# Another order of the setup work of a cross-attention and FFN kernel: first q product between the halves of the DCA keys, head products ahead of the DCA scales, output bias and DCA values further back

## What is computed

```python
def _ln(t, w, b):
    m = jnp.mean(t, axis=-1, keepdims=True)
    v = jnp.var(t, axis=-1, keepdims=True)
    return (t - m) * jax.lax.rsqrt(v + 1e-6) * w + b

# y = ctx_1024; the last 16 of its 128 tokens are the "DCA" tokens
kv_dca = (y_dca @ Wkv_dca + bkv_dca).reshape(b, 16, 2, H, HD)
k_dca, v_dca = _ln(kv_dca[:, :, 0], kn_dca_w, kn_dca_b), kv_dca[:, :, 1]
q = _ln((x @ Wq + bq).reshape(b, s1, H, HD), qn_w, qn_b)      # x: layernorm of the input
kv = concatenate([y_main @ Wk + bk, y_main @ Wv + bv]).reshape(b, s2, H, 2 * HD)
k, v = _ln(kv[..., :HD], kn_w, kn_b), kv[..., HD:]
ctx = softmax(q k^T * HD**-0.5) v  +  softmax(q k_dca^T * HD**-0.5) v_dca
x = x_in + ctx @ Wo + bo
# FFN: activations, kernel (per column) and bias fake-quantised to 8 bits
y = relu(xq @ kq + bq);  out = x + fake_quant(y)              # xq: layernorm(x), quantised per row
```

## Time and profile before

| | us |
|---|---|
| median of 3 runs | 368.0 (364.89 to 369.49) |
| the profiled execution | 367.36 |
| its span on the core | 365.6 |
| PE busy | 320.0 (88%) |
| VectorE (DVE) busy | 314.6 (86%) |
| ScalarE (ACT) busy | 222.5 (61%) |
| GpSimd (POOL) busy | 173.3 (47%) |
| mean granted TensorE clock | 0.966 |

### The profile page before, as it was taken

One profiled execution on the slowest core, in us unless ns is written; L12 is line 12 of the kernel. 1 busy time (PEld: TensorE's weight loads), 2 busy tenths in 40 slices (PEclk: granted clock), 3 DMA queues, 4 the chain that ended last, 5 costly groups with the idle time before them and its releaser, 6 DMA issues.

```text
span 365.6 us, 7583 instructions
## 1 busy us (share of the span) xinstructions
PE 320.0 (88%) x2338; PEld 258.6 (71%) x2353; DVE 314.6 (86%) x804; ACT 222.5 (61%) x444; POOL 173.3 (47%) x261
## 2 busy tenths in 40 slices
PE   1499889799999999999999999999999999797732
PEld 0345557688878888888888888888888888595620
DVE  2987999899989999999999989999989898946664
ACT  3357986466666767676667666767676756542401
POOL 5301512337373838373738382828282827251620
PEclk9999999899999999999999999999999999959985
DMA  7870368526171919182919091919291809070002
GB/s 267 254 281 1 70 138 146 120 58 136 31 162 43 180 42 178 43 168 55 179 40 182 27 195 33 186 35 155 68 185 35 151 16 163 25 122 2 29 0 86
DMA packets 36451, 39.14 MB, mean 107 GB/s; under 512 B 8760, under 2 KB 27452, under 8 KB 36412
## 3 DMA queue, kind: packets, MB, share of 16 engines
q1 hardware_dynamic: 36044, 38.40, 48.9%
q10 hardware_dynamic: 368, 0.27, 0.3%
HBM read 17.15 MB, written 4.72 MB: 60 GB/s over the span
## 4 chain that ended last, share of the span: by engine, by line
PE 49%; DMA 10%; SPq 8%; issue 6%; ACT 3%; DVE 3%; POOL 0%; ACTq 0%; DVEq 0%
PE bank L1328 24%; DMA q_stack<-q_lo 10%; SPq L376 8%; PE bank L1445 7%; PE bank L1414 4%; PE bank L1601 4%; PE bank L1611 2%; PE bank L1425 2%; PE bank L1426 2%; PE bank L1468 2%; PE bank L1498 2%; ACT k_hi L611 1%; PE bank L1460 1%; DVE finals L1050 1%; PE bank L1503 1%
## 5 line engine op out<-in xcount | busy, mean ns | idle before, releaser
L1445 PE MATMUL bank<-v_aug,prob_store 128*128 128x66 f32 x512 | 70.7, 284 | 3.4 <-ACT prob_store L749 3.4
L1445 PEld LDWEIGHTS bank<-v_aug,prob_store 128*128 128x128 f32 x512 | 66.5, 200 | 5.7 <-ACT prob_store L749 4.5
L516 POOL TENSOR_TENSOR k_lo<-wkv_raw,k_hi 128x448 f16<-128x448 f32 x16 | 16.7, 1043 | 110.8 <-issue 102.9
L1061 DVE TENSOR_REDUCE neg_max<-bank 128x4 f32<-128x448 f32 (+1 forms) x128 | 45.1, 415 | 5.6 <-PE bank L1414 5.4
L760 ACT ACTIVATE wkv_raw<-bank,affine 128x448 f32<-128x448 f32 (+1 forms) x32 | 22.4, 748 | 42.4 <-PE bank L1498 42.1
L749 ACT ACTIVATE prob_store<-bank,exp_scale 128x512 f32<-128x512 f32 x64 | 41.7, 677 | 7.4 <-PE bank L1426 7.3
L535 POOL TENSOR_TENSOR finals<-seg_out 128x128 f32<-128x128 f32 x64 | 34.5, 547 | 17.1 <-DVE seg_out L1074 16.9
L1425 PE MATMUL bank<-q_stack,k_stack 128*128 128x128 f16 x256 | 34.7, 223 | 1.9 <-ACT maxT L611 1.9
L1426 PE MATMUL bank<-maxT,sel 128*128 128x128 bf16 x256 | 34.5, 222 | 0.0
L1425 PEld LDWEIGHTS bank<-q_stack,k_stack 128*128 128x128 f16 x256 | 26.9, 107 | 6.1 <-issue 3.9
L1074 DVE TENSOR_TENSOR seg_out<-bank,rden 128x256 f32<-128x256 f32 x64 | 27.1, 424 | 3.5 <-POOL finals L535 1.4
(11 more groups left out here) (213 smaller groups left out, 871.8 us busy)
## 6 DMA issues: line engine op xcount, KB each, us to landing
x_in<-in_x SPq DMA_DIRECT2D x16, 256.0 KB, 3.0
q_stack<-q_hi SPq DMA_DIRECT2D x32, 128.0 KB, 3.6
q_stack<-q_lo SPq DMA_DIRECT2D x32, 128.0 KB, 4.8
k_stack<-k_hi SPq DMA_DIRECT2D x32, 128.0 KB, 3.3
k_stack<-k_lo SPq DMA_DIRECT2D x32, 128.0 KB, 4.3
out<-finals SPq DMA_DIRECT2D x16, 256.0 KB, 2.7
y_in<-in_ctx SPq DMA_DIRECT2D x16, 128.0 KB, 2.7
y_dcaT<-in_x SPq DMA_DIRECT2D x8, 256.0 KB, 3.7
```

The source lines that it names most:

```text
L1061: v.tensor_reduce(neg_max[:, HG * gr:HG * (gr + 1), seg], s4[:, :, lo:hi], AX.X, ALU.max, negate=True).then_inc(max_ready.sem, 1)
L1445: last = mm(bank[6 + gr % 2][:, VW * h:VW * (h + 1)], probs[:, gr % 2, h], v_aug[:, Bt.parity, HG * gr + h], start=True, stop=True)
```

## The change

No operation is added, removed or resized; instructions of the setup change places within their engines' queues. On TensorE the q product of batch 0 goes between the two halves of the DCA keys; the output bias goes from the head of t=-1 to behind the fk column transposes, the DCA transposes go behind the k and the q product of batch 1, the DCA values behind the first scores, and at t=0 (`N.second()`) PE waits for the DCA copies. On ACT the copies and squares of the DCA keys are parted, the Ln and Exp of the DCA heads go between the normalisation of k and of q, and the first DCA step and the first |fk| behind q_hi. On VectorE the affine columns and the head products of batch 0 go ahead of the DCA sums and scales, and the output bias behind the head products of batch 1. On SyncE and GpSimd nothing changes place.

```diff
--- before.py
+++ after.py
@@ -661,10 +661,12 @@
                 for c, into in ((2, prob_store[:, 1]), (3, fk_mag)):
                     s.activation(into, fk_raw[:, c], ACT.Abs).then_inc(fkmag_ready.sem, 1)
 
+            def setup_copied(j):
+                act.wait_ge(kvdca_ready.sem, j + 1)
+                copy(kv_dca[:, j, 0], bank[4 + j][:, :]).then_inc(kvdca_copied.sem, 1)
+
             def setup_squares():
-                for j in range(2):
-                    act.wait_ge(kvdca_ready.sem, j + 1)
-                    copy(kv_dca[:, j, 0], bank[4 + j][:, :]).then_inc(kvdca_copied.sem, 1)
+                setup_copied(1)
                 act.wait_ge(kvdca_copied.sem, 2)
                 s.activation(dca_sq[:], kv_dca[:, :, 0], ACT.Square).then_inc(dcasq_ready.sem, 1)
 
@@ -770,6 +772,7 @@
                     if not N.second():
                         heads(N)
                     if N.first():
+                        setup_squares()
                         act.wait_ge(tiles_made.sem, 7)
                     act.wait_ge(*v_ready.of(N))
                     if N.has(2):
@@ -789,12 +792,15 @@
                         setup_keys()
                         setup_weights()
                 if N is not None:
+                    normed(kT_ready, 6, MAIN, 2, k_n, kn_ready, klo_ready)
                     if N.first():
-                        setup_dca(0)
-                    normed(kT_ready, 6, MAIN, 2, k_n, kn_ready, klo_ready)
+                        setup_heads()
                     normed(qT_ready, 2, P, 0, q_n, qn_ready, qlo_ready)
                     high(k_hi, k_n, kn_ready, MAIN, kstack_in, khi_ready)
                     high(q_hi, q_n, qn_ready, P, qstack_in, qhi_ready)
+                    if N.first():
+                        setup_dca(0)
+                        setup_columns()
                 if Bt is not None:
                     act.wait_ge(*maxP_ready.of(Bt))
                     if Bt.has(1):
@@ -807,11 +813,9 @@
                         for n, made in ((1, bank[1]), (0, bank[7])):
                             act.wait_ge(bias_made.sem, 2 - n)
                             copy(bias_full[:, n], made[:, :]).then_inc(bias_copied.sem, 1)
-                        setup_squares()
+                        setup_copied(0)
                         squared_keys()
                         token_statistics()
-                        setup_columns()
-                        setup_heads()
                 if N is not None and N.first():
                     setup_dca(1)
                 if L is not None and not L.second():
@@ -843,9 +847,9 @@
                 if N is not None and N.first():
                     heads(A)
                     setup_wo()
-                    setup_values()
                     setup_ffn()
                     setup_selectors()
+                    setup_values()
                 if D is not None and not final(D):
                     act.wait_ge(*yrnd_ready.of(D))
                     if D.has(1):
@@ -1160,12 +1164,10 @@
                                         ).then_inc(taillo_ready.sem, 1)
                 if N is not None and not N.second():
                     if N.first():
-                        setup_scales()
-                        setup_dca(0)
+                        setup_affine()
                     head_products(N)
                     if N.first():
-                        setup_dca(1)
-                        setup_pairs()
+                        setup_squares()
                 if Bt is not None and Bt.first():
                     setup_ffn_bias()
                 if A is not None:
@@ -1190,10 +1192,11 @@
                 if A is not None:
                     if A.first():
                         low_queries()
+                        biased_keys()
                         setup_norms()
-                        setup_affine()
-                        biased_keys()
-                        setup_squares()
+                    elif N.first():
+                        setup_scales()
+                        setup_dca(0)
                 if Bt is not None and Bt.first():
                     low_query()
                     low_output()
@@ -1244,8 +1247,9 @@
                     v.reciprocal(f_small[:, 13:14], row_scale(D)).then_inc(yscale_steps.sem, 1)
                 if N is not None:
                     if N.first():
+                        setup_dca(1)
+                        setup_pairs()
                         biased_keys()
-                        setup_output()
                         setup_columns()
                 if Bt is not None and final(Bt):
                     normalise(0)
@@ -1294,6 +1298,7 @@
                         head_means(A)
                         setup_maxima()
                         head_products(A)
+                        setup_output()
                     maxima(0)
                     maxima(1)
                 if C is not None and final(C):
@@ -1341,14 +1346,13 @@
                                   ident[:])
                 last.then_inc(ydcaT_ready.sem, 1)
 
-            def setup_keys():
+            def setup_keys(j):
 
                 pe.wait_ge(ydcaT_copied.sem, 1)
                 pe.wait_ge(wd_centred.sem, 1)
-                for j in range(2):
-                    for c in range(YC):
-                        mm(bank[4 + j][:, :], y_dcaT[:, j, c, :], wd_raw[:, c, 0, :], start=c == 0, stop=False)
-                    mm(bank[4 + j][:, :], ones3[0:3, :], bias_split[:, 2], start=False, stop=True).then_inc(kvdca_ready.sem, 1)
+                for c in range(YC):
+                    mm(bank[4 + j][:, :], y_dcaT[:, j, c, :], wd_raw[:, c, 0, :], start=c == 0, stop=False)
+                mm(bank[4 + j][:, :], ones3[0:3, :], bias_split[:, 2], start=False, stop=True).then_inc(kvdca_ready.sem, 1)
 
             def setup_values():
                 pe.wait_ge(out_bias_ready.sem, 1)
@@ -1449,8 +1453,6 @@
                 if Bt is not None:
                     if Bt.first():
                         pe.wait_ge(sel_made.sem, 2)
-                if N is not None and N.first():
-                    setup_output()
                 if A is not None:
                     p = A.parity
                     pe.wait_ge(*y_loaded.of(A))
@@ -1492,7 +1494,8 @@
                     if N.first():
                         pe.wait_ge(affine_ready.sem, 2)
                         pe.wait_ge(bv_sum_ready.sem, 1)
-                        setup_dca(0)
+                    if N.second():
+                        pe.wait_ge(kvdca_copied.sem, 4)
                     pe.wait_ge(*kt_ready.of(N))
                     for c in range(XC):
                         last = tr(bank[6][:, P * c:P * c + MAIN], k_t[0:MAIN, P * c:P * (c + 1)], ident[0:MAIN, 0:MAIN])
@@ -1502,8 +1505,6 @@
                     for c in range(XC):
                         last = tr(bank[2][:, P * c:P * (c + 1)], q_t[:, P * c:P * (c + 1)], ident[:])
                     last.then_inc(qT_ready.sem, 1)
-                    if N.first():
-                        setup_dca(1)
                 def transposed_maxima():
                     pe.wait_ge(*maxhi_ready.of(Bt))
                     pe.wait_ge(*maxlo_ready.of(Bt))
@@ -1523,8 +1524,9 @@
                     split_product(bank[3][0:MAIN, :], yT_hi, yT_lo, wk_hi, wk_lo, range(YC), MAIN).then_inc(k_ready.sem, 1)
                     if A.first():
                         setup_biases()
-                        setup_keys()
-                        setup_columns()
+                        setup_keys(0)
+                    elif N.first():
+                        setup_dca(0)
                 if Bt is not None and not Bt.first():
                     transposed_maxima()
                 if A is not None:
@@ -1550,9 +1552,13 @@
                         pe.wait_ge(wqlo_ready.sem, 2)
                     split_product(bank[2][:, :], xT_hi, xT_lo, wq_hi, wq_lo, range(XC // 2, XC), P
                                   ).then_inc(q_ready.sem, 1)
+                    if A.first():
+                        setup_keys(1)
+                        setup_columns()
                 if N is not None and N.first():
+                    setup_dca(1)
                     setup_columns_wide()
-                    setup_values()
+                    setup_output()
                     setup_scales()
                 if Bt is not None and Bt.first():
                     first_shifted()
```

## The result

The changed kernel takes 373.4 us (median of 6 runs, 369.6 to 376.2), the kernel before in the same measurement 368.7. The ratio is 1.0124, interval 1.0071 to 1.0177: slower by 1.2%, inside the 2% band. The forecast was 371.5 and a range of 367 to 375.5. The profiled execution took 376.16; this one and one of 375.2 had lower mean granted clocks (0.946 and 0.936) than the other four (0.952 to 0.956), and ratios leave such slow executions out. A second trace of each kernel (e10, e12) helps with that.

What follows compares the result with a forecast made beforehand. TensorE was taken to bound the repeating 18.29 us steps, so only t=0's start could move: +0.7 (VectorE) + 5.5 - 2.4 (TensorE) = +3.75 us, forecast 371.5 us, range 367 to 375.5.

Steps and rivals of the forecast that it cites:

- The q product and the head products: Batch 0 setup: head means 4.8 us earlier, at 28.55; q's head product 4.7 us earlier, at 33.15.
- The new wait on ACT: ACT, between k and q normalisation of batch 0: Ln and Exp wait for DCA sums, giving back 0.9 us.
- the way through q_hi: Batch 0 path from q normalisation through stack transfers to first scores: q_hi 3.9 us earlier, at 36.58.
- The transfers: SyncE stack transfers before the first scores: possible gain 3.8 us, worth something only if TensorE reaches the scores then.
- case D: Rival: waits shorter than counted, TensorE held by its own work alone, +1.2 us, 369; chance 0.13.
- The term of +3.75: Y transposes of t=0 start at 56.8 instead of 53.03, passed on whole to the total.
- The cover named for the late tokens: Batch 3 tokens land 0.4 us late; 2 us before VectorE needs the exponentials hides it, cost 0.
- a fall behind the 2.8 us wait: TensorE before the fk column transposes: clock likely falls from about 44.4, costing 0 if short, 2.2 us if long.
- the short case: Low clock of 3.4 us hits only the output bias, hidden by VectorE's wait: cost 0, total 371.5.
- case A: The step-by-step sum holds: +2.5 to +4.5 us, total 370 to 372; chance 0.60.
- Case B: Rival: long low clock behind the new idle ahead of t=0, +5.9 us, 373.3 to 375, to 377.5; chance 0.15.
- Case C: Rival: the clock no longer falls where it did, notably the late long fall, total 366.5; chance 0.12.

Runs made afterwards that it cites:

- e10: The changed kernel again, unaltered, for a second trace; 373.1 us (10 runs), ratio 1.0102.
- e12: The kernel before again, unaltered, for a second trace; 372.0 us (a single run).
- e4: The kernel before with only the q product of batch 0 moved between the halves of the DCA keys; 372.9 us, ratio 1.0124.
- e7: The changed kernel with Ln and Exp of the DCA heads behind q_hi instead of between k and q normalisation; 375.5 us (a single run).
- e3: The changed kernel with |fk| of the first two chunks back on ACT at t=-2, behind the token statistics; 370.5 us, ratio 1.0075.
- e5: The changed kernel with one TensorE swap, output bias ahead of the fk column transposes; 376.0 us (a single run).
- e2: The changed kernel with output bias ahead of the fk column transposes and DCA values right behind them, VectorE and ACT parts moved too; 368.5 us (10 runs), ratio 1.0033.
- e11: The changed kernel with 20 and 24 unread matmuls filling TensorE's two waits of t=0; 370.4 us (4 runs), ratio 1.0103.
- e1: The changed kernel with output bias and DCA values back in their old places on all engines; 370.0 us (10 runs), ratio 1.0100.
- e6: The changed kernel with SyncE issuing batch 3's tokens ahead of its wait for the DCA copies and the store; 373.0 us (4 runs).
- e9: The changed kernel with output bias, values, two |fk| chunks and selectors earlier, and the FFN bias in VectorE's wait; 366.8 us (12 runs), ratio 0.9976.

## Why the prediction was right, and where it was off

**The q product and the head products.** Head means at 29.17 (forecast 28.55), in e10 28.30; the 0.6 is the landing of the bias rows, 18.97 for 18.35. That 4.8 us at the head means only come if VectorE's queue is turned too is shown by e4, where the q product alone makes them 2.7 later.

**The new wait on ACT.** 0.69 us idle was seen, 0.9 was given for it. Its price on the path is nothing or less: e7 takes it away and is slower (one trace). I had listed it among the losses of the way through q_hi; that way was not the path in the changed kernel any more.

**The transfers.** The last key transfers went out at 42.21 (forecast 41.2) instead of 45.02; the first scores did not wait for them. The gain was off the path, as said.

**ACT, VectorE, TensorE.** Forecast and measured: squares of q 46.46 and 46.95; output bias done 51.85 and 52.20; wait ahead of the columns 2.8 and 2.79; y transposes 56.8 and 57.17 (56.12 in e10). e3 moved ACT's share and the end by the same 1.96. e5 showed that TensorE's own order in front of the output bias is hidden, which is against case D. e2 showed that the output bias in the wait and the values in front of the column transposes, moved together, take back 3.0. The term of +3.75 is 3.2 over two traces of each kernel.

**SyncE.** The cover named for the late tokens was VectorE's row. The tokens went out at 60.50 instead of 53.58, behind the store, and ACT waited 1.22 us for them where 0.4 was forecast. The sum put nothing on TensorE for the same wait, and TensorE waited 1.70 us for the first exponentials (2.06 in e10), where it had waited 0.39. With the waits filled (e11) the step is only 0.24 longer than in e1 and e2, where the tokens are in time: as such the wait is nearly free. With the clock falling behind it the step is 1.6 to 3.3 us longer than in e6, where the wait is gone.

**The clock, where the sum was off.** The forecast looked for a fall behind the 2.8 us wait and found 0 for a short one. In the first trace it was so (3.4 us, hidden); in e10 there was none. What failed is that t=0 was then passed on "whole", with its 3.5 us of low clock taken as fixed. It has 10.0 and 13.5 in the changed kernel, 3.5 and 7.0 in the other. Over the four traces the y transposes are 3.2 us later, the step is 2.6 longer and the rest of the span 0.4 shorter, 5.3 in all, where the medians are 4.7 and 4.6 apart. So the term +3.75 was 0.6 too large by these traces, and the missing term is the step.

**The cases.** The measured 373.4 lies above case A's 370 to 372, which had 0.60, and at the lower end of B's 373.3 to 375, which had 0.15. Case B had the right kind, a long low clock on top, and the wrong place. The upper part of the range was there for that other fall, so that the total stayed well inside it is partly luck. Case C asked for the late fall near the end of the run to go away. From 300 to 360 us the mean grant is 0.86 in both traces before, 0.89 in the first of the changed kernel and 0.97 in e10: there most of it did go, and the span behind the step is 2.9 us shorter than in the first trace, while the step is 1.7 longer. The prediction quotes the Trainium skill, page "TensorE: Matmul & The Clock Gate", Part 1: activity releases the throttle. The trace does not bear out the short case that the prediction made of it for the falls in t=0: from 66 to 80 us TensorE was busy 13.23 of 14 us, at a mean grant of 0.63.

**What stays open.** That a step with more low clock is longer is shown by the table. That TensorE's waits bring the fall rests on e11, one trace, and on where the falls begin. The length of a wait does not decide alone: 1.71 us had no fall behind it in e1 and e2 and one in e9, 2.8 us one in the first trace of the changed kernel and none in e10. The order of the change does seem to make the longer falls likelier, by way of the late tokens: it moves the long wait to the first weighing, and e6 moves it back. But that is one execution for most kernels, and the total of e6 is no lower. How much of the 4.7 us it explains is not shown, and what makes a fall last is not known.

## What to carry to other kernels

When setup instructions are pushed behind one another in several queues, follow each engine's queue to its next wait for another engine: a result made 4 us earlier is worth nothing if the same queue then waits for work that another engine has put behind it. Long pieces of TensorE work (here 3.4 us each) belong into a wait that exists, with their consumer queued so that it need not stand for them; e2 took back 3 us of its first interval so. A late transfer must be covered on every engine that waits for it in turn: here VectorE had the cover and TensorE did not. Judge such a change by intervals between two fixed instructions in the trace, since the totals of the kernel before alone scatter from 362.4 to 372.1 us.

## What was not expected of the hardware

The time TensorE spends at 1.2 GHz in the window around t=0 came as 0, 3.5, 7.0, 10.0 or 13.5 us in thirteen of fourteen traces (in e5 it was 11.5, of which 3.2 were from an earlier fall). In the changed kernel it ran on while the engine was busy 13.23 of 14 us. A wait of 2.8 us had a fall behind it in one trace of the changed kernel and none in the other.
